# First routing, entry into attention and state product of a macaron block re-ordered on one Trainium2 core

## What is computed

```python
def ffn(x, gate_w, gate_b, w1, w2):
    probs = softmax(x @ gate_w.T + gate_b, axis=-2)       # over the tokens
    vals, idx = top_k(probs over tokens, 8)               # per sequence and expert
    tok = x[idx]
    merged = einsum('bked,bke->bed', tok, vals)           # one row per expert
    h = gelu([merged, 1] @ w1);  o = [h, 1] @ w2
    return scatter_add(o * vals, idx)

def attention(x):
    q, k, v = exp(x @ Wq.T + bq), exp(x @ Wk.T + bk), x @ Wv.T + bv
    kv, k1 = cumsum(k v^T), cumsum(k)                     # over the tokens, per head
    return ((q kv) / (q . k1)) @ Wo.T + bo

x = x + 0.5 * ffn(layernorm(x));  x = x + attention(layernorm(x));  x = x + 0.5 * ffn(layernorm(x))
```

## Time and profile before

| | us |
|---|---|
| median of 3 runs | 2403.8 (2402.45 to 2406.37) |
| the profiled execution | 2402.62 |
| its span | 2400.9 |
| busy: PE / PEld / DVE / ACT / POOL | 2027.0 / 1187.7 / 733.1 / 822.0 / 646.4 |
| gate / first expert pass / entry to attention | 0 to 132.5 / to 979.3 / to about 1060 |
| attention / second expert pass | to about 1748 / to the end |

### The profile page before, as it was taken

One profiled execution on the slowest core, in us unless ns is written; L12 is line 12 of the kernel. 1 busy time (PEld: TensorE's weight loads), 2 busy tenths in 40 slices (PEclk: granted clock), 3 DMA queues, 4 the chain that ended last, 5 costly groups with the idle time before them and its releaser, 6 DMA issues.

```text
span 2400.9 us, 44276 instructions
## 1 busy us (share of the span) xinstructions
PE 2027.0 (84%) x18716; PEld 1187.7 (49%) x18716; DVE 733.1 (31%) x1229; ACT 822.0 (34%) x1539; POOL 646.4 (27%) x803
## 2 busy tenths in 40 slices
PE   5789999999999999889999999999775666666555
PEld 4556566566656665666666666666521111111111
DVE  6631111111111111266777677677420000000002
ACT  6731111111111111257777777777500000000000
POOL 8510000000000000067777777777411000000002
PEclk9899999999999999999999999999887777777888
DMA  9989999999999999654545454544399999999995
GB/s 373 339 343 368 390 403 390 384 400 380 420 400 404 392 399 386 210 212 155 160 144 168 147 157 148 164 141 159 134 400 422 425 424 424 425 424 424 425 424 212
DMA packets 130709, 762.22 MB, mean 317 GB/s; under 512 B 21156, under 2 KB 21156, under 8 KB 77264
## 3 DMA queue, kind: packets, MB, share of 16 engines
q1 hardware_dynamic: 118736, 701.35, 74.3%
q10 hardware_dynamic: 9216, 50.34, 5.0%
q0 software_dynamic: 2560, 7.70, 0.8%
HBM read 648.09 MB, written 105.91 MB: 314 GB/s over the span
## 4 chain that ended last, share of the span: by engine, by line
PE 44%; DMA 38%; POOL 8%; ACT 4%; issue 3%; DVE 3%; POOLq 0%; SPq 0%; ACTq 0%; DVEq 0%
PE ps L297 40%; DMA big<-in_L_ffn_w 37%; PE ps L301 3%; POOL s L1397 1%; POOL big L1394 1%; POOL big L1368 1%; POOL big L1399 1%; ACT big L1237 1%; ACT ps L1221 1%; DVE big L627 1%; POOL s L1379 1%; DVE big L305 1%; POOL big L665 1%; POOL big L1361 1%; PE ps L427 0%
## 5 line engine op out<-in xcount | busy, mean ns | idle before, releaser
L297 PE MATMUL ps<-big 128*32 128x512 f32 (+5 forms) x13776 | 1009.7, 424 | 264.8 <-DMA big<-in_L_ffn_w 233.9
L297 PEld LDWEIGHTS ps<-big 128*32 128x32 f32 (+2 forms) x13776 | 384.3, 128 | 808.7 <-issue 399.9
L305 DVE TENSOR_TENSOR big<-ps,big 128x128 f32<-128x128 f32 (+3 forms) x373 | 338.1, 932 | 749.1 <-PE ps L763 570.0
L297 PE MATMUL ps<-wth,xth 128*128 128x512 f32 x768 | 310.2, 404 | 0.0
L806 ACT COPY big<-ps 128x512 f32<-128x512 f32 x64 | 37.5, 586 | 768.5 <-PE ps L297 768.5
L297 PE MATMUL ps<-wth,xtl 128*128 128x512 f32 x768 | 300.3, 391 | 0.0
L297 PE MATMUL ps<-wtl,xth 128*128 128x512 f32 x768 | 300.3, 391 | 0.0
L1386 POOL TENSOR_SCALAR big<-big 128x1 f32<-128x1 f32 x64 | 12.2, 190 | 903.9 <-ACT ps L1221 898.6
L297 PE MATMUL ps<-wo,s 128*128 128x512 f32 x768 | 211.1, 410 | 3.4 <-ACT big L1285 1.9
L301 PE MATMUL ps<-big 128*128 128x128 f32 x1032 | 167.4, 296 | 28.6 <-ACT big L575 12.4
L950 ACT ACTIVATE big<-ps,big 128x512 f32<-128x512 f32 x128 | 88.2, 689 | 262.0 <-PE ps L297 260.1
(11 more groups left out here) (124 smaller groups left out, 1777.6 us busy)
## 6 DMA issues: line engine op xcount, KB each, us to landing
big<-in_L_ffn_w SPq DMA_DIRECT2D x256, 2048.0 KB, 22.0
p_scratch<-big ACTq DMA_DIRECT2D x64, 768.0 KB, 10.0
big<-p_scratch SPq DMA_DIRECT2D x64, 768.0 KB, 5.5
big<-in_L_attn_x SPq DMA_DIRECT2D x68, 256.0 KB, 2.9
xt_scratch<-big SPq DMA_DIRECT2D x16, 1024.0 KB, 8.2
big<-xt_scratch SPq DMA_DIRECT2D x16, 1024.0 KB, 15.5
x_weight_scratch<-big SPq DMA_DIRECT2D x64, 256.0 KB, 3.3
out_x<-big SPq DMA_DIRECT2D x64, 256.0 KB, 3.4
```

Of the source, the lines that this page charges most:

```text
L297: return nc.tensor.matmul(o, l, r, start=start, stop=stop, skip_group_check=True)
L305: return nc.vector.tensor_tensor(o, p, q, op)
```

## The change

Gate: every merge step stands one group later, and a group's transposes and logits stand ahead of its merge transposes; the scaled means are one 128x4 instruction on VectorE; the loads of the biases move ahead of SyncE's loop over groups (and share the semaphore `d_bias`, for all of which the logits wait); four weight units instead of two lie in the tail, and the last round's weights stand ahead of two merge reductions on VectorE.

Entry: the last tile's three units are spread between centring and outer units, the third behind outer 5; the table load and exponential of the K bias stand ahead of outer 0's copy on ScalarE; the sixth copy stands behind the first tile's square; sequences 4 to 7 of `OS` are written in the loop at n=1 to 4; the three chunk loads are issued one at a time at n=2, 6 and 10; the last tile's store stands at n=0.

Attention: the state product of tile n+1 stands behind the values of tile n, in bank 0 instead of 3; its addition stands behind the reciprocal and the routing steps of tile n; the K transposes wait for that addition.

```diff
@@ gate_sp
             for g in range(4, 7):
                 load_x(g)
+            load_biases(sp)
...
-                if g == 9:
-                    load_biases(sp)
@@ gate_pe
-                for b in second(g, 6) + first(g, 5):
+                for b in second(g, 7) + first(g, 6):
                     pe.wait_ge(s_mg, b)
                     pe.wait_ge(s_mt, b - b % 2 + 2)
                     merge_end_pe(pe, b, 7)
+                transposes_pe(pe, g)
+                if g:
+                    logits_pe(pe, g - 1)
+                for b in first(g, 5) + second(g, 6):
+                    pe.wait_ge(s_pr3, b)
+                    merge_tokens_pe(pe, b, 6)
                 for b in first(g, 4) + second(g, 4):
                     pe.wait_ge(s_mt, b - b % 2)
                     pe.wait_ge(s_mg, b - b % 2)
                     merge_transpose_pe(pe, b, 5 + b % 2 * 2)
-                transposes_pe(pe, g)
-                if g:
-                    logits_pe(pe, g - 1)
-                for b in first(g, 4) + second(g, 5):
-                    pe.wait_ge(s_pr3, b)
-                    merge_tokens_pe(pe, b, 6)
@@ logits_act
-            act.wait_ge(d_bias, 64)
+            act.wait_ge(d_bias, 16 * 11)
@@ gate_dve
                     dve.wait_ge(s_rs4, h + 1)
+                    dve.wait_ge(s_nma, acts(max(h - 3, 0)))
+                    nc.vector.scalar_tensor_tensor(out=NMG[h % 4], in0=MVG[h % 4][:, :, 0], scalar=-1.0,
+                                                   in1=RSG[h % 4], op0=ALU.mult, op1=ALU.mult).then_inc(s_nm4, 1)
...
             round_dve(dve, 4)
+            round_weights(dve, 4)
             merge_end_dve(dve, 4, 7)
-            merge_end_dve(dve, 5, 0)
-            round_weights(dve, 4)
-            weights_dve(dve, 0, 1)
-            merge_end_dve(dve, 6, 1)
-            weights_dve(dve, 1, 2)
+            merge_end_dve(dve, 5, 4)
+            weights_dve(dve, 0, 4)
+            merge_end_dve(dve, 6, 5)
@@ gate_pool
-                for j in on_act(g):
-                    nc.gpsimd.tensor_scalar(NMG[g % 4][:, j:j + 1], MV_[:, j, 0:1], RS_[:, j:j + 1], -1.0, ALU.mult,
-                                            ALU.mult).then_inc(s_nm4, 1)
@@ attention_sp
-            for h in range(2):
-                outer_sp(sp, h)
+            sp.wait_ge(s_o, 2)
+            sp.wait_ge(d_pst[0], 16 * (NT // 2))
+            sp.wait_ge(d_pst[1], 16 * (NT // 2 - 1))
+            for b in range(4):
+                sp.dma_start(OS[b][96:128, :], O[quad(b), 0, :]).then_inc(d_os[0], 16)
+            for u in range(3):
+                sp.wait_ge(s_os, u + 1)
+                for b in range(4):
+                    sp.dma_start(OS[b][32 * u:32 * u + 32, :], OW[u][quad(b), :]).then_inc(d_os[0], 16)
             for n in range(-2, NT + 2):
+                if 1 <= n < 5:
+                    outer_sp(sp, n + 3)
...
-                if n == 1:
+                if n in (2, 6, 10):
                     sp.wait_ge(s_ow, 6)
-                    for g in range(4 * E, 4 * E + 3):
-                        load_chunk(sp, g)
+                    sp.wait_ge(s_pu, 3 * NT)
+                    load_chunk(sp, 4 * E + (n - 2) // 4)
@@ attention_pe
-            center_pe(pe)
-            for v in range(5):
+            ahead_pe(pe, NT - 1, (0,))
+            center_pe(pe, 0)
+            ahead_pe(pe, NT - 1, (1,))
+            outer_pe(pe, 0)
+            center_pe(pe, 1)
+            for v in range(1, 5):
                 outer_pe(pe, v)
...
-                if live and c < 7:
-                    pe.wait_ge(s_v, n + 1)
-                    pe.wait_ge(s_at, n)
-                    for g in range(4):
-                        for r in range(4):
...
+                if n == 0:
+                    state_pe(0)
...
                     t.then_inc(s_av, 1)
+                    if n + 1 < NT:
+                        state_pe(n + 1)
...
                 if n == -2:
                     outer_pe(pe, 5)
+                    ahead_pe(pe, NT - 1, (2,))
...
                     if m == 0:
                         pe.wait_ge(s_os, 6)
+                    else:
+                        pe.wait_ge(s_kva, kvs(m + 1))
@@ attention_act
+            act.wait_ge(s_bk, 1)
+            nc.scalar.activation(BK, BK, ACT.Exp).then_inc(s_eb, 1)
+            outer_act(act, 0)
             act.wait_ge(s_xsl, NT)
             nc.scalar.copy(WOH, WO).then_inc(s_woh, 1)
-            for v in range(6):
+            for v in range(1, 5):
                 outer_act(act, v)
-            act.wait_ge(s_bk, 1)
-            nc.scalar.activation(BK, BK, ACT.Exp).then_inc(s_eb, 1)
...
+                if n == -1:
+                    outer_act(act, 5)
+                if n == 0:
+                    store_act(act, NT - 1)
@@ attention_dve
-                if live and c < 7:
-                    dve.wait_ge(s_kv, kvs(n) + 1)
...
+                if live and n + 1 < NT:
+                    state_dve(n + 1)
```

More of the change, by code:

```diff
@@ L591, in gate_act @@
                     if i == 1:
-                        for b in first(g, 4) + second(g, 4):
+                        for b in first(g, 5) + second(g, 5):
                             merge_transpose_act(act, b, 5 + b % 2 * 2)
@@ L597, in gate_act @@
                     logits_act(act, g - 1)
-                for b in first(g, 4) + second(g, 5):
+                for b in first(g, 5) + second(g, 6):
                     merge_tokens_act(act, b, 6)
             round_act(act, 3)
+            merge_transpose_act(act, 4, 5)
+            merge_transpose_act(act, 5, 7)
             logits_act(act, NG - 1)
-            merge_tokens_act(act, 5, 6)
+            merge_tokens_act(act, 4, 6)
             merge_transpose_act(act, 6, 5)
             round_act(act, 4)
+            merge_tokens_act(act, 5, 6)
             merge_tokens_act(act, 6, 6)
-            weights_act(act, 0, 1)
+            weights_act(act, 0, 4)
             merge_transpose_act(act, 7, 5)
-            weights_act(act, 1, 2)
             merge_tokens_act(act, 7, 6)
@@ L637, in gate_dve @@
                     round_weights(dve, r)
-                for b in first(g, 5) + second(g, 6):
+                for b in first(g, 6) + second(g, 7):
                     merge_end_dve(dve, b, 7)
@@ L857, in experts_dve, with merged_dve @@
                     weight_dve(dve, e - 16)
+            if p == 1:
+                for h in range(2):
+                    merged_dve(dve, p, h)
+        def merged_dve(dve, p, h):
             dve.wait_ge(s_sel, 8 * p + 8)
             dve.wait_ge(d_b2, 64 * p + 64)
-            for h in range(2):
-                tt(O[:, h, :], ps[:, 6 + h, :], B2, ALU.add).then_inc(s_o, 1)
+            tt(O[:, h, :], ps[:, 6 + h, :], B2, ALU.add).then_inc(s_o, 1)
         def weights_pe(pe, lo, hi):
@@ L916, in split_dve, with ahead_pe @@
                ALU.subtract).then_inc(s_xsl, 1)
-        def ahead_pe(pe, t):
+        def ahead_pe(pe, t, units=range(3)):
             if t == 0:
@@ L921, in ahead_pe @@
             pe.wait_ge(s_xsl, t + 1)
-            for u in range(3):
+            for u in units:
                 q = 3 * t + u
@@ L939, in store_act, with ahead_act @@
             act.dma_start(pd[t], PST[t % 2]).then_inc(d_pst[t % 2], 16)
-        def ahead_act(act, t):
+        def ahead_act(act, t, units=(0, 1)):
             if t + 1 < NT:
                 split_act(act, t + 1)
-            if t:
+            if t and 0 in units:
                 store_act(act, t - 1)
             act.wait_ge(d_pst[t % 2], 16 * (t // 2))
-            for u in range(2):
+            for u in units:
                 q = 3 * t + u
```

149 lines of the change are left out of this document (83 added, 66 removed).

## The result

| | before | after |
|---|---|---|
| median of 5 runs each | 2402.45 us (2401.27 to 2406.37) | 2379.04 us (2377.71 to 2388.39) |
| the profiled execution (its span) | 2402.62 (2400.9) | 2381.70 (2380.0) |

The ratio is 0.9908 with a 95% interval of 0.9888 to 0.9928: faster by 17 to 27 us. A second set of five runs of the same kernel gave 2383.01 against 2403.65, ratio 0.9917 (0.9904 to 0.9930). The forecast was 2392 with a range of 2378 to 2402: the sign and the range hold, the gain is about twice the forecast 11.6.

What follows compares the result with a forecast made beforehand. Bound: a chain across engines in the gate, TensorE in attention, transfers in the last expert pass. Gate -3.5, entry with stall -14.65 and body +6.5 sum to -11.6: 2391.0 by the profiled execution, 2392 as median, range 2378 to 2402.

Steps and rivals of the forecast that it cites:

- The body's +6.5: Attention tiles: state product moved behind values costs about 0.85 us per eight tiles, +6.5 us in all, ends 0 and +13.
- not touched but for two weight units: First expert pass: unchanged except two fewer weight units in expert 0, -1.1 us, counted in the gate's sum.
- Entry: Last expert to attention's tile 0: earlier outer and first prefix products, no long idle, last store moved; -7.75 us.
- Stall: Early attention: chunk loads issued one at a time end the x2 addition's wait for a store; -6.9 us.
- where logits or merge work fill the first part anyway (c=1, 4, 5) about 0: Attention tiles c=1, 4, 5, scores to values: moving the state product out changes the tile by about 0.
- The rule of the Trainium skill on narrow matmuls: State product's 32 matmuls: at least about 25 ns start to start, 0.8 us where exposed; forecast said the trace contradicts it.
- rival 4: Attention: K transposes wait for VectorE's addition in all tiles; 42 tiles x 0.69 = 29 us, 2421; chance 0.06.
- Gate: Start of the kernel up to the expert pass: -2.6 - 1.3 - 1.1 + 1.5 = -3.5 us, ends -7 and +2.
- "-2.6" for the means: Gate: scaled means moved from GpSimd to VectorE make each pair of groups 0.33 us shorter, times eight, -2.6 us.
- "-1.3" for the tail: Gate's tail: two merge reductions on VectorE now come behind the last round's weights, for which TensorE waited; -1.3 us.
- "+1.5" for the biases: Gate: biases land near 26 to 28 us, making the first logits and ScalarE late; +1.5 us, between 0 and 5.
- the merge steps one group later: Gate: merge transposes one group later remove TensorE's wait for merge weights; costed at nothing, up to 5.5 us once.

## Why the prediction was right and wrong

The profiled executions differ by 20.9 us, 9.3 more than the forecast 11.6: 4.1 of this lie in the body, 1.8 ahead of expert 1, 1.9 in the rest of the first pass and 2.0 behind attention, less 0.5 in entry and stall. Two terms of the sum failed. The body's +6.5 was +1.9 to +2.4, mainly since c=1, 4 and 5 were put at "about 0". And the first expert pass, "not touched but for two weight units", was given no change of clock in its first product, which was worth -1.7. The 3.9 of the last two stretches lie within what these stretches vary from profile to profile (786.0 to 791.8 and 674.2 to 680.7 us).

**Entry: right.** -7.6 measured for -7.75, and 70.9 to 71.7 us from the last expert to tile 0 in every profile with the new order, 79.3 with the old (80.85 once). c(0) is held by the row transfers (1.64 us), as the forecast had put between its two ends. Part of the match is luck: counted from the last expert c(0) came 2.3 us earlier, where 3.2 was forecast, and from the first prefix matmul to tile 0 1.4 was won, where 0.75 was (of which the four passes give 4 x 0.30 = 1.2, not the 1.1 written there). No run takes the steps of the entry apart.

**Stall: right.** -6.9 forecast, -6.9 in the kernel before with nothing else changed, -6.5 in the changed one, -8.6 when the edit is taken back there.

**Body: right mechanism, one term mis-sized.** Of the +6.5 for 64 tiles, 1.9 to 2.4 came. The failing step is "where logits or merge work fill the first part anyway (c=1, 4, 5) about 0". One tile with c=5, from its scores to the next (the 32-column matmuls are the state product, those from 32x32 the values), before

```profile
1255.54 1.17 PE L297 MATMUL ps<-big 32*128 32x128 f32 x32
...
1258.16 0.46 PE L297 MATMUL ps<-big 128*32 128x32 f32 x32
...
1260.43 3.16 PE L297 MATMUL ps<-big 32*32 32x128 f32 x72
...
1266.89 1.17 PE L297 MATMUL ps<-big 32*128 32x128 f32 x32
```

and after:

```profile
1235.38 1.17 PE L297 MATMUL ps<-big 32*128 32x128 f32 x32
...
1239.67 3.45 PE L297 MATMUL ps<-big 32*32 32x128 f32 x104
...
1246.44 1.17 PE L297 MATMUL ps<-big 32*128 32x128 f32 x32
```

By the starts of scores and values in the two timelines these tiles win: at c=4 scores to values went from 4.47 to 4.04, at c=1 and 5 from 4.88 to 4.29. In a part that TensorE fills, taking the product out gives back 0.43 to 0.60, more than the 0.39 that I had as its price, and behind the values it costs 0.29. So c=1 and 5 are 0.3 shorter each and c=4 0.16, some 0.75 in eight tiles where nothing was forecast, and c=6 is 0.60 shorter (forecast 0.39). c=2 came as worked out (+0.65 for +0.6); c=3 was worse (+0.82 for +0.15): a wait of 1.02 for GpSimd's low part stands there. With the addition early 0.71 of it stays, so that it comes back from c=2's delay is shown for a part of it only. Eight tiles are +0.6 in most sequences and -0.4 in two, the second and the sixth, where c=3 had waited 0.92 for GpSimd before too. The rule of the Trainium skill on narrow matmuls ("TensorE: Matmul & The Clock Gate", section "Wait — 56ns, not 53.3ns?"), by which 32 of them would take 0.8 us, an estimate, does not hold here, behind values no more than ahead of them: 32 more added 0.29 us. K transposes waiting in every tile (rival 4) did not happen; the wait is in c=2 and c=3 of five of the eight sequences.

**Gate: right sum at its end by luck, wrong parts.** Forecast -2.4 without the weight units; in the two profiles -2.4, and over four profiles with the old and seven with the new gate -3.0 (133.9 to 130.9). But of the parts "-2.6" for the means is nothing, "-1.3" for the tail is -3.2 in one profile, and "+1.5" for the biases is about +2.5 (they landed near 29 us; the terms given, 17.5 and 6 to 8, make 23.5 to 25.5, not the 26 to 28 written there). What is left over, some -2.5, would be the merge steps one group later, which I had costed at nothing with 5.5 as the most; that was not tried by itself. At the last expert little of this is left: with the tail alone it comes at 950.92, in the nine profiles with the whole changed gate at 949.0 to 957.5, mean 951.5, and in the four with the old tail at 957.7 to 959.4. So the tail alone, by its one profile, is worth as much there as the whole gate.

**The first expert pass: a term that was missing.** Two fewer units in expert 0 gave -1.26 (expert 0 to 1 takes 28.49, not 29.75), for -1.1 forecast. The first product took 3.64 in all nine profiles with the changed gate and 5.34 in all five with the order before, the new tail alone among these: -1.7. Which step of the gate this hangs on was not found. The other -1.9 up to the last expert is wandering: 786.0 to 791.8 us from expert 1 to the last one, with no order between old and new gates.

**Behind attention: chance.** 674.2 to 680.7 us in fourteen profiles, by when the last chunk lands and at which clock the last products run: its products start 639.3 to 642.3 us after tile 63, and from there to the end it is 34.7 to 38.7 us. The first profile of the changed kernel happens to be the shortest. With its second profile, 4.5 us longer there, the same sum is -19.6.

So the gain, 20 to 23 us by the two medians, is 14 from entry and stall as forecast, about 7 from gate and first pass for 3.5, less a cost of 2 for 6.5 in the body; the few microseconds left are within what the stretch behind attention varies.

## What to carry to other kernels

When a step moves between two stretches, price both stretches by what ends last in each, tile by tile: a product taken out of a stretch that its own engine fills gives back its full pace. Look then at what waits for the moved step's result on the next engine, and put that small operation ahead of the long ones in the queue: here one 0.29 us addition on VectorE, put ahead of the routing steps and not behind them in two of eight tiles, was worth 7 us, more than the move. Split a bulk load that shares a queue with stores on the path into pieces spaced apart, here one every fourth tile; and where the last stage runs on transfers, compare two kernels by stretches of the timeline, since their totals differ by several microseconds from clock and transfers alone.

## What the runs showed of the hardware

The same 32 matmuls behind the same steps took 3.64 us or 5.0 to 6.6 us, by the granted clock: it was 1.00 through the first product of the changed kernel (130 to 134 us), and 0.50, the lower of its two levels (1.2 GHz), from 134 to 136 us in that of the kernel before. In the gate it was 3.64 in nine profiles of nine with the changed order and 5.34 in five of five with the order before or one part of the new one alone, while the steps of the last 5 us were alike in the changed kernel and with the tail alone. Forty idle transposes behind attention were followed by matmuls at the full clock and gave nothing at the end, because the transfers behind were the bound. The sixteen-matmul group of the last chunk, at 1.92 or 3.64, lies between the last landing and the end, and with the four matmuls behind it makes 3.5 us of difference between runs of one kernel.
